# Causal attention with a quantised gate on Trainium2: the gate's closures run at blocks 0, 1, 3, 4 instead of 0, 2, 4, 5

## The chip, the cores and the metric

One Trainium2 chip, 8 cores, one program on all of them. Core 2b and core 2b+1 compute batch element b, each one half of the output features (8 of the 16 heads). The cores share nothing but memory bandwidth. The metric is the device time of the slowest core in microseconds.

## The reference

Shapes: x is 4 x 4096 x 1024 (float32), 16 heads of 64, FFN weight 1024 x 1024 int8.

```python
xn = layernorm(x)                                   # over 1024
qkv = xn @ W                                        # 1024 x 3072
a = softmax(mask(q @ k.T / 8)); s = a @ v           # causal, 16 heads
x_q = clip(round(xn / (amax(|xn|) / 127)))          # per row, int8
g = silu((x_q @ weight_q.T) * x_scale * weight_scale + bias)
out = x + s * g
```

The reference's reshape of k (heads x 64 x sequence read as heads x sequence x 64) is a fixed rearrangement of k, which the kernel makes when it writes `kTa`.

## The kernel before

**Order by hand.** The kernel writes one list of instructions for each engine (`Sched.emit`) with explicit semaphore waits, and replays the lists. So the order of `emit` calls in Python is the order in each engine's queue; nothing is reordered later. An instruction that waits holds up all that its engine has behind it.

**Phases.** First (up to about 590 us) a pass over the 32 row tiles of 128: statistics, normalised tile, transposes, all of k (into `kTa`), and for the first 4 chunks of 512 rows also their quantised tiles. Then attention, chunk by chunk: `emit_attention_chunk(c)` for c = 0 to 7, 512 query rows each. For the chunks from 4 on, tile work is done inside attention: `a_substeps(tc)` gives a list of steps, with `s` (load x and normalise on POOL), `qa`/`qb` (quantise one half tile: four DVE instructions, L428, L430, L433, L436), `p` (transposes on PE, L481 and L486, into the PSUM buffer `pt`, evacuated by DVE at L491), then the row of scales (L512), v (L551), and the FFN (L581, evacuated by DVE L586, then POOL L590, ACT L596, DVE L601). The q projections (L534, evacuated by ACT L540) are a list of their own. The four projections all use the one PSUM buffer `pm`.

**One unit.** Inside a chunk the loop runs over P = 0 to 3 (a pair of heads); this text calls one pass the unit (c,P). A unit has `njb = 4c + 4` blocks `jb` of 128 keys. For each block, in this order in the code: a closure of the previous unit's gate, if this block is in `pops_at`; from block 3 on, the AV pair of the block three before (L788 and L792, into `Oa` and `Ob`, from `eT`); the score pair (L729 and L735; L742 to L767 for the four diagonal blocks) into `sT[par]`, of which there are two; the exp on ACT (L774) from `sT` to one of three `eT`; then `pump()`, which emits usually one step of the tile work, while there is any. The last three AV pairs close the unit. `Oa` and `Ob` are one buffer each, so AV0 of the next unit waits (`O_rd`) until the gate has read them.

**The gate of a unit** is four closures put into `att["pend_gate"]` at the end of the unit and popped in the next one:
- ga1 (`emit_gating_a1`): ACT copies the two rows of softmax sums from `Oa` and `Ob` to `rows` (L821, L824); DVE multiplies `Oa` and `Ob` by the gate `gT` into `wpr` (L827, L831).
- ga2 (`emit_gating_a2`): PE turns the sum rows into columns with fp32 matmuls of one column into `pm` (L842, L846), waiting for the row copies and for `pm`; DVE takes the reciprocal, `linvT` (L852), which frees `pm`.
- gb1 (`emit_gating_b1`): POOL issues the DMA of the residual `xres` (L859).
- gb2 (`emit_gating_b2`): PE transposes `wpr` into `pt` (L870); DVE makes `outs` in eight products (L878, L884), which frees `pt`; POOL issues the output DMA (L891).

`drain_pre` (chunk c, P = 0, block 4c - 1) and `drain_full` (at P = 1) emit whatever of a chunk's own tile work is not out yet. The number of steps that `pump` emits does not depend on the gate. The gate of unit (7,3) is drained after the loop.

Of the kernel before, what the change touches and what calls it, by code (L numbers as in the profile page):

```python
# [67 lines left out]
def build_program(S=4096):  # L68
# [628 lines left out]
    def emit_attention_chunk(c, pump, close_open, drain_pre, drain_full):  # L697
        for P in range(NPAIR):
            if P == 1:
                drain_full()  # L700
            njb = 4 * c + 4
# [5 lines left out]
                if pend_av:  # L707
                    pend_av.pop(0)()

            pops_at = (0, 1, 2, 3) if njb <= 4 else (0, 2, 4, 5)  # L710
            for jb in range(njb):
                if P == 0 and jb == 4 * c - 1:
                    drain_pre()
# [302 lines left out]
    for c in range(NTC):  # L1016
# [37 lines left out]
        def close_open():  # L1054
            drain_open()
        emit_attention_chunk(c, pump, close_open, drain_pre, drain_full)
    while ia["k"] < len(flatA):
        stepA()
# [84 lines left out]
```

How the kernel before makes its waits and increments, by code:

```python
    def replay(self, eng, handle, sems):  # L47
        seen = {}
        own = self.OWN.get(eng)
        prior = 0
        for waits, fn, inc in self.ops[eng]:
            allw = list(waits)
            if own is not None and prior > 0:
                allw.append((own, prior))
            for s, v in allw:
                if seen.get(s, 0) >= v:
                    continue
                handle.wait_ge(sems[s], v)
                seen[s] = v
            ins = fn(handle)
            if inc is not None:
                s, amt = inc
                ins.then_inc(sems[s], amt)
                if s == own:
                    prior += amt
```

## Time and profile before

| | |
|---|---|
| median of 2 runs | 1580.31 us (1579.34 to 1581.28) |
| the profiled execution | 1573.33 us |
| its span, slowest core (core 7) | 1571.8 us |
| spans of the eight cores | 1562.5 to 1571.8 us |
| mean granted TensorE clock, all cores | 0.799 to 0.809 of full speed |
| PE busy | 1112.5 us (71%) |
| ACT busy | 719.3 us (46%) |
| DVE busy | 571.8 us (36%) |
| POOL busy | 299.7 us (19%) |
| DMA | 47.46 MB, mean 30 GB/s |

The rows further down name an engine, a line and an operation with its tiles (out<-in). "[0.45 <-PE sT L735]" at the end of a line of the timeline is the idle time of that engine ahead of the instruction and what ended it. "x2" at the end is the number of instructions merged in one line.
### The profile page before, as it was taken

The numbers are of one execution on the slowest core, as the hardware profiler recorded it, in microseconds if no ns is written. First come the engines' busy times: TensorE is split into PE (matmuls) and PEld (weight loads), VectorE is DVE, ScalarE is ACT, GpSimd is POOL, SyncE is SP. The second block draws the span as 40 slices with busy tenths as digits, with TensorE's granted clock in tenths as the row PEclk, the third lists the DMA queues.
The fourth block names the chain that finished last, engine by engine and source line by source line (L and its number), as shares of the span: only waits on it lengthen the run. The fifth ranks groups of instructions, "written<-read, shape, count | busy, mean of one in ns | idle before, by whom it ended". The sixth has DMA issues, their size and how long they took to land.

```text
span 1571.8 us, 17863 instructions; the slowest of 8 cores (1562.5 to 1571.8 us)
## 1 busy us (share of the span) xinstructions
PE 1112.5 (71%) x5200; PEld 456.6 (29%) x5200; DVE 571.8 (36%) x1086; ACT 719.3 (46%) x905; POOL 299.7 (19%) x412
## 2 busy tenths in 40 slices
PE   0336546445465558996987987888698888888886
PEld 0112212212221214443443433333233333332332
DVE  0484382562735553237237227222721001110000
ACT  0121220211311113553454475467447878888886
POOL 1440430411505451122022022011200000000000
PEclk9956757659586656867988998898798999999998
DMA  7110010000101211021011011001000000000000
GB/s 118 49 33 13 21 34 0 30 24 1 47 7 54 67 47 53 28 67 54 7 48 41 8 48 53 8 21 41 21 8 21 14 14 14 15 22 13 7 14 20
DMA packets 24463, 47.46 MB, mean 30 GB/s; under 512 B 4272, under 2 KB 7472, under 8 KB 24368
## 3 DMA queue, kind: packets, MB, share of 16 engines
q0 software_dynamic: 8816, 20.98, 5.4%
q1 hardware_dynamic: 15552, 25.34, 5.3%
q8 instruction: 44, 0.72, 0.2%
q14 instruction: 51, 0.42, 0.1%
HBM read 40.54 MB, written 8.39 MB: 31 GB/s over the span
## 4 chain that ended last, share of the span: by engine, by line
PE 34%; DVE 26%; ACT 18%; issue 8%; POOL 6%; DMA 6%; DVEq 1%; ACTq 0%; POOLq 0%; SPq 0%
ACT eT L774 16%; PE pm L551 4%; PE Oa L788 4%; PE pm L534 4%; DVE t_r L430 3%; DVE t_b L433 3%; PE Ob L792 3%; DMA xst<-x 3%; PE sT L729 3%; PE pm L581 3%; DVE t_g L428 2%; DMA w8n<-w 2%; PE pm L842 2%; DVE bnst L240 2%; PE pm L846 2%
## 5 line engine op out<-in xcount | busy, mean ns | idle before, releaser
L774 ACT ACTIVATE eT<-sT 128x1024 bf16<-128x1024 f32 (+1 forms) x576 | 548.9, 953 | 271.7 <-PE sT L735 144.8
L788 PE MATMUL Oa<-eT,v_aug 128*65 128x512 bf16 (+1 forms) x576 | 240.1, 417 | 2.9 <-DVE wpr L831 0.2
L792 PE MATMUL Ob<-eT,v_aug 128*65 128x512 bf16 (+1 forms) x576 | 227.8, 400 | 0.0
L729 PE MATMUL sT<-qT,kTa 64*128 64x512 bf16 x448 | 183.4, 418 | 38.7 <-ACT eT L774 37.6
L735 PE MATMUL sT<-qT,kTa 64*128 64x512 bf16 x448 | 186.2, 424 | 0.0
L891 POOL DMA_DIRECT2D out<-outs x32 | 24.2, 756 | 762.2 <-DVE outs L884 705.2
L827 DVE TENSOR_TENSOR wpr<-Oa,gT 64x512 bf16<-64x512 f32 x32 | 21.8, 683 | 363.4 <-PE Ob L792 362.6
L301 PE MATMUL sT<-Wqk,xnK 128*128 128x512 bf16 x256 | 112.0, 616 | 47.3 <-ACT xnK L289 42.8
L729 PEld LDWEIGHTS sT<-qT,kTa 64*128 64x128 bf16 x448 | 40.3, 94 | 225.3 <-issue 222.6
L788 PEld LDWEIGHTS Oa<-eT,v_aug 128*65 128x65 bf16 x576 | 67.7, 118 | 106.8 <-issue 95.5
L551 PE MATMUL pm<-Wv,xnq 128*128 128x512 bf16 x256 | 74.8, 445 | 21.9 <-DVE v_aug L558 17.6
L581 PE MATMUL pm<-xnq,wqT 128*128 128x512 bf16 x256 | 70.2, 424 | 24.6 <-DVE g1s L586 20.5
L281 PE MATMUL pt<-idb_s,xnbf 128*128 128x128 bf16 x128 | 17.3, 283 | 96.4 <-POOL xqbf L269 83.8
L289 ACT ACTIVATE xnK<-pt 128x1024 bf16<-128x1024 bf16 x32 | 32.8, 1024 | 100.0 <-PE pt L281 93.9
L240 DVE BATCH_NORM_STATS2 bnst<-xst 128x6 f32<-128x512 f32 x64 | 44.4, 694 | 90.0 <-DMA xst<-x 84.5
L590 POOL TENSOR_SCALAR t_b<-g1s,wscb,biab 128x512 f32<-128x512 f32 x32 | 24.6, 767 | 271.5 <-DVE g1s L586 271.5
L305 ACT ACTIVATE ktmp<-sT 128x512 bf16<-128x512 f32 x32 | 19.1, 598 | 124.6 <-PE sT L301 124.6
L842 PE MATMUL pm<-idf_s,rows 1*128 1x1 f32 x256 | 50.8, 265 | 34.7 <-DVE wpr L831 22.8
L878 DVE SCALAR_TENSOR_TENSOR outs<-pt,linvT,xres 128x64 f32<-128x64 bf16 x128 | 36.2, 283 | 107.0 <-PE pt L870 93.5
L534 PE MATMUL pm<-xnq,Wqk 128*128 128x512 bf16 x256 | 63.5, 393 | 16.0 <-ACT qT L540 8.7
L792 PEld LDWEIGHTS Ob<-eT,v_aug 128*65 128x65 bf16 x576 | 69.9, 121 | 7.2 <-issue 0.5
L301 PEld LDWEIGHTS sT<-Wqk,xnK 128*128 128x128 bf16 x256 | 32.6, 136 | 106.7 <-issue 106.0
(122 smaller groups left out, 1571.6 us busy)
## 6 DMA issues: line engine op xcount, KB each, us to landing
xst<-x SPq DMA_DIRECT2D x96, 256.0 KB, 2.9
xres<-xr POOLq DMA_DIRECT2D x32, 256.0 KB, 3.6
out<-outs POOLq DMA_DIRECT2D x32, 256.0 KB, 2.8
Wqk<-wq POOLq DMA_DIRECT2D x1, 1024.0 KB, 13.4
Wqk<-wk POOLq DMA_DIRECT2D x1, 1024.0 KB, 24.7
Wv<-wv POOLq DMA_DIRECT2D x1, 1024.0 KB, 29.6
w8n<-w POOLq DMA_DIRECT2D x4, 256.0 KB, 2.6
wscb<-wsc SPq DMA_DIRECT2D x4, 0.5 KB, 6.3
```

The source lines that it names most:

```text
L240: sc.emit("vector", lambda v, buf=buf, h2=h2, bnst=bnst: v.bn_stats(bnst[:, 6 * h2:6 * h2 + 6], xst[:, 512 * buf:512 * buf + 512]), waits= ...
L301: c_mm = sc.emit("tensor", lambda t, kk=kk, xK=xK, slotA=slotA: t.matmul(slotA, xK[:, kk, :], Wqk[:, kk, 512:1024], start=(kk == 0), stop= ...
L430: sc.emit("vector", lambda v, off=off, inv=inv, txn=txn: v.scalar_tensor_tensor(t_r[:], txn[:, off:off + 512], inv, t_g[:], ALU.mult, ALU. ...
L534: c_mm = sc.emit("tensor", lambda t, kk=kk, f=f: t.matmul(pm[:], Wqk[:, kk, 128 * f:128 * f + 128], xnq[:, kk, :], start=(kk == 0), stop=( ...
L551: c_mm = sc.emit("tensor", lambda t, kk=kk, vs=vs: t.matmul(pm[:], xnq[:, kk, 128 * vs:128 * vs + 128], Wv[:, kk, :], start=(kk == 0), sto ...
L581: c_mm = sc.emit("tensor", lambda t, kk=kk, oc=oc: t.matmul(pm[:], wqT[:, kk, 128 * oc:128 * oc + 128], xnq[:, 8 + kk, :], start=(kk == 0) ...
L729: t.matmul(sT[par][:, o:o + w], kTa[0:64, P, 128 * jb:128 * jb + 128], qT[P][0:64, qb + o:qb + o + w], start=True, stop=True), waits=w0)
L735: qb=qb: t.matmul(sT[par][:, 512 + o:512 + o + w], kTa[64:128, P, 128 * jb:128 * jb + 128], qT[P][64:128, qb + o:qb + o + w], start=True, ...
L774: s.activation(eT[pe3][:].rearrange("p (b n) -> p b n", b=2)[:, :, o:o + w], sT[par][:].rearrange("p (b n) -> p b n", b=2)[:, :, o:o + w], ...
L788: sc.emit("tensor", lambda t: t.matmul(Oa[:, o:o + w], v_aug[:, jb, 65 * hA:65 * hA + 65], eT[pe3][:, o:o + w], start=(jb == 0), stop=(jb ...
L792: c_av = sc.emit("tensor", lambda t: t.matmul(Ob[:, o:o + w], v_aug[:, jb, 65 * hB:65 * hB + 65], eT[pe3][:, 512 + o:512 + o + w], start=( ...
L842: c_lt = sc.emit("tensor", lambda t, it=it: t.matmul(pm[0:128, 2 * it:2 * it + 1], rows[64:65, 128 * it:128 * it + 128], idf[64:65, 64:65] ...
```

## The change

The blocks at which the four closures of the previous unit's gate are popped. Units of chunk 0 (4 blocks) keep theirs; the 28 units of chunks 1 to 7 pop ga1, ga2, gb1, gb2 at blocks 0, 1, 3, 4, where it was 0, 2, 4, 5.

```diff
@@ -707,7 +707,7 @@
                 if pend_av:
                     pend_av.pop(0)()
 
-            pops_at = (0, 1, 2, 3) if njb <= 4 else (0, 2, 4, 5)
+            pops_at = (0, 1, 2, 3) if njb <= 4 else (0, 1, 3, 4)
             for jb in range(njb):
                 if P == 0 and jb == 4 * c - 1:
                     drain_pre()
```

So ga2 stands in PE's queue behind the scores of block 0 (and the step pumped there) instead of behind those of block 1; gb1 and gb2 are each one block and one pumped step earlier in the queues of POOL, PE and DVE.

## Rows read from the trace of the kernel before

**Rows 1.** The page's costliest groups: busy, mean ns, idle before and its releaser
```profile
L774 ACT ACTIVATE eT<-sT 128x1024 bf16<-128x1024 f32 (+1 forms) x576 | 548.9, 953 | 271.7 <-PE sT L735 144.8
```

**Rows 2.** Busy us (instructions) by window, then PE clock, DMA share, GB/s
```profile
849.00:988.00 139.00, 114.22 (x605) 51.15 (x603) 59.94 (x108) 74.73 (x85) 21.58 (x28) 0.87 0.10 31
...
1440.00:1572.00 132.00, 107.44 (x506) 39.55 (x504) 15.36 (x44) 99.18 (x104) 5.24 (x7) 0.90 0.05 15
```

**Rows 3.** Timeline of ACT, start of unit (7,1): start, us, engine, line, operation
```profile
1440.12 0.59 ACT L821 ACTIVATE rows<-Oa 1x512 f32<-1x512 f32 x1 [0.57 <-PE Ob L792]
...
1441.48 2.14 ACT L774 ACTIVATE eT<-sT 128x1024 bf16<-128x1024 f32 x2
1444.08 1.02 ACT L774 ACTIVATE eT<-sT 128x1024 bf16<-128x1024 f32 x1 [0.45 <-PE sT L735]
1445.61 1.02 ACT L774 ACTIVATE eT<-sT 128x1024 bf16<-128x1024 f32 x1 [0.51 <-PE sT L735]
1447.14 2.18 ACT L774 ACTIVATE eT<-sT 128x1024 bf16<-128x1024 f32 x2 [0.51 <-PE sT L735]
```

**Rows 4.** Timeline of PE, the same stretch
```profile
1440.13 0.38 PE L729 MATMUL sT<-qT,kTa 64*128 64x512 bf16 x1
...
1441.64 0.35 PE L842 MATMUL pm<-idf_s,rows 1*128 1x1 f32 x2 [1.13 <-DVE wpr L831]
...
1443.20 0.36 PE L846 MATMUL pm<-idf_s,rows 1*128 1x1 f32 x2
1443.49 0.43 PE L729 MATMUL sT<-qT,kTa 64*128 64x512 bf16 x1
...
1444.85 0.60 PE L729 MATMUL sT<-qT,kTa 64*128 64x512 bf16 x1
...
1446.92 0.47 PE L870 MATMUL pt<-idb_s,wpr 128*128 128x128 bf16 x4
```

**Rows 5.** Windows behind the gates run in (7,1) and (7,2)
```profile
1443.56:1447.12 3.56, 3.56 (x13) 0.81 (x14) 0.21 (x1) 2.11 (x3) 0.00 (x0) 0.52 0.00 0
1447.12:1479.00 31.88, 27.86 (x134) 8.92 (x134) 2.26 (x8) 27.39 (x28) 1.49 (x2) 1.00 0.06 17
...
1481.20:1488.10 6.90, 6.90 (x28) 3.76 (x29) 0.21 (x1) 4.02 (x5) 0.00 (x0) 0.51 0.01 2
```

**Rows 6.** Timeline of ACT, start of unit (7,2)
```profile
1484.47 1.02 ACT L774 ACTIVATE eT<-sT 128x1024 bf16<-128x1024 f32 x1 [1.77 <-PE sT L735]
...
1488.97 2.14 ACT L774 ACTIVATE eT<-sT 128x1024 bf16<-128x1024 f32 x2 [0.41 <-PE sT L735]
```

**Rows 7.** The waits: who waited for whom, us in total, times, longest
```profile
PE pt L481 <- DVE outs L884: 30.0, 5, 7.1
...
PE pm L842 <- DVE wpr L831: 22.8, 20, 1.7
```

**Rows 8.** Timeline of DVE and PE, start of unit (4,0)
```profile
947.03 0.48 DVE L428 TENSOR_SCALAR t_g<-t_xn,statq 128x512 int32<-128x512 f32 x1
...
948.80 0.60 PE L729 MATMUL sT<-qT,kTa 64*128 64x512 bf16 x1
...
950.09 0.21 DVE L852 RECIPROCAL linvT<-pm 128x8 f32<-128x8 f32 x1
...
959.67 0.26 PE L481 MATMUL pt<-idb_s,xnK 128*128 128x128 bf16 x1 [6.19 <-DVE outs L884]
...
961.20 0.69 DVE L491 COPY xnq<-pt 128x1024 bf16<-128x1024 bf16 x1 [1.68 <-PE pt L486]
```

**Rows 9.** Timeline of PE, start of unit (3,2)
```profile
893.63 1.89 PE L581 MATMUL pm<-xnq,wqT 128*128 128x512 bf16 x8 [0.69 <-DVE g1s L586]
...
897.07 0.35 PE L842 MATMUL pm<-idf_s,rows 1*128 1x1 f32 x2 [1.56 <-DVE g1s L586]
...
900.69 3.57 PE L581 MATMUL pm<-xnq,wqT 128*128 128x512 bf16 x8
```

**Rows 10.** The page's DMA issues: count, KB each, median us to landing
```profile
xres<-xr POOLq DMA_DIRECT2D x32, 256.0 KB, 3.6
```

## The prediction

> **What bounds the kernel now.** I read the page's groups first, then busy time by stage, then the waits, then the timeline around single gates. "Unit (c,P)" is one pass of the `jb` loop; "the gate" of a unit is its four closures, which run inside the next unit. scN, expN, AVN are the scores, exp and AV pair of jb = N.
>
> The exp (L774) is the costliest group: 548.9 us busy in 576 instructions, 271.7 us idle before them [rows 1]. By stage [rows 2]: in the last 132 us (chunk 7) ACT is busy 99.2 us and PE 107.4, nothing else is near, and DVE has 44 instructions; between 849 and 988 us (chunk 3) the tile work of a later chunk is mixed in, DVE has 108 instructions and 59.9 us. So there are two kinds of stretch: exp-bound units, and units in which PE and DVE hand tiles to each other.
>
> In an exp-bound unit ACT hardly waits away from the two ends: exps follow each other every 1.07 us [rows 3], and in the 31.88 us behind the start of unit (7,1) 28 of them are busy for 27.39 us, PE at full clock [rows 5]. The start of a unit is different. The last AV ends, ACT copies the two sum rows (0.59 us each), then runs exp0 and exp1 from 1.36 us on [rows 3]. PE does sc0 and sc1 at once, then stands until it may run ga2: its 16 fp32 matmuls start 1.52 us after the first row copy and are over at about 3.4 [rows 4]. The wait is 1.13 us here, and of this kind there are 20, together 22.8 us [rows 7]. sc2 comes after ga2, so exp2 waits 0.45 us; then the clock is at its lower level (0.52 of 2.4 GHz, that is 1.2) for some 3.5 us [rows 5], PE needs 1.5 us a block, and exp3 and exp4 wait 0.51 us each [rows 3].
>
> **The change, part by part.** Nothing is added or removed. In the 28 units with c >= 1 three closures come one block earlier; the three gates inside chunk 0 and the drained last gate are as before. ga1 stays.
>
> *ga2 from ahead of sc2 to ahead of sc1, exp-bound unit.* It can't start sooner: the row copies and the two wpr products end at the same moments, and its start follows them, not sc1 [rows 3, 4]. So sc1 (0.22 us at full clock) moves from a hole in PE to behind ga2, and exp1, which ran back to back with exp0, now waits. I walk unit (7,1), zero being 1440.12:
> - before: sc1 0.01, ga2 1.52 to 3.37, sc2 3.37, exp2 3.96, sc3 4.73, exp3 5.49, exp4 7.02, gapless from there [rows 3, 4].
> - after: ga2 1.52 to 3.37, sc1 3.37, exp1 3.96 to 4.98. sc2 follows at 3.7 and exp2 at 5.03 (ACT decides), AV0 takes its 1.0 us (the 1.36 between sc2 and sc3 less the score pair), sc3 stands at 5.2, exp3 at 6.1. The wpr transposes (L870, 0.3 us at full clock, 0.4 at half) now come before AV1 instead of before AV2; AV1 takes 1.0, so sc4 is at about 7.1 and exp4 at 7.65, by then at full clock. exp4 before: 7.02. Loss 0.63 us.
> - unit (7,2) is the other form: the low clock lasts 6.9 us instead of 3.56 [rows 5] and exp2 waits 1.77 [rows 6]. Counted from the start of its old exp2, exp5 starts at 4.50 [rows 6]. The same walk puts exp1 at 0, exp2 at 1.07, sc3 1.3, exp3 2.1, sc4 3.3, exp4 4.0, exp5 5.1: loss 0.6 us.
>
> What is lost in ACT isn't given back, since ACT runs gapless behind it. There are 13 such gates (run in (3,3), (4,2), (4,3), from (5,2) on all): 13 x 0.62 = 8.1 us. Bounds of one: at least 0.22 us (one score pair at full clock, if ACT absorbs all else), at most 1.07 us (a whole exp pitch: exp2's old place taken by exp1, with nothing won back afterwards).
>
> *The same, PE-bound short units.* The gates run in (1,1), (1,2), (1,3) and (2,3) have no tile work either, but PE sets their pace, largely at half clock. The idle stretch of PE grows by sc1, which is then done at either clock: 0.22 to 0.53 us; I take 0.45: 1.8 us.
>
> *Units with tile work in their first blocks* ((2,0), (3,0), (4,0), (5,0) start it, (2,1) and (3,1) end it). Here DVE sets the pace. In (4,0) DVE starts the first quantisation right after wpr, at 947.03, while PE is in ga2; the reciprocal linvT comes after four quantisation instructions, at 950.09 [rows 8]. After the change linvT is queued ahead of them and waits for ga2's end (sc2 starts at 948.80): four instructions start at about 949.1 instead, 2.1 us later, of which 0.3 is linvT itself, no longer in its old slot: DVE loses 1.8. Against this, gb2's eight products (L878, L884) go ahead of the third quantisation (four instructions, 3.1 us, by the distance from the first to linvT) instead of behind it. The tile transposes L481 that wait for them lose less (6.19 us before), and DVE no longer idles 1.68 us before it can evacuate them (L491) [rows 8]. Net 0.1 us lost by these rows, up to 0.5 where that gap is shorter. PE is some 1.3 us earlier at L481, but its next transposes wait for L491, which DVE does no earlier. I take 0.3 for each of the four and 0.3 for the two others together: 1.5 us.
>
> *Units with projections between the first blocks* (five gates: (1,0), (2,2), (3,2), (4,1), (5,1)). ga2 shares pm with them, and each user waits for the evacuation of the one before. In (3,2): L581, sc1, a second L581 at 893.63, 1.56 us of wait, ga2, sc2, the third L581 at 900.69 [rows 9]. After: L581, ga2 at 893.6 in the place of the second L581, sc1, the second L581 at about 896.5 (behind linvT, which stands behind L601 on DVE), sc2, its evacuation, the third L581 at about 899.5: 1.2 us won. I take -1.2 for it and -0.5 for (1,0), which has the same order; (2,2) and (5,1) lose the score pair, 0.25 each; (4,1) is even. Together -1.2 us.
>
> *gb1 and gb2.* The distance from the residual's DMA issue to its user stays one block, in POOL's queue the issue passes at most one step, and without tile work it is issued long before. Cost nothing beyond what is counted; if POOL is behind (it may be with projections) DVE waits for the landing, 3.6 us after the issue [rows 10], as before; both ends of that cost stay under one landing.
>
> **Sum:** 8.1 + 1.8 + 1.5 - 1.2 = 10.2 us. The profiled execution took 1573.3 us (span 1571.8), 7 us under the median of the runs; I add the sum to that median of 1580.3: 1590.5.
>
> **Rivals.**
> - *The stall behind outs is what counts (not slower).* PE waits 30.0 us in five places for L884 to free pt [rows 7]. gb2 one quantisation earlier frees it 3 us sooner, so 15 us could be won: 10.2 - 15 = -5: 1575.5. For it: these are PE's longest waits, and exp waits with them. Against: DVE has hardly a gap behind them, so PE only waits at the next transposes. It turns the sign once more than 2 us of each stays won. Chance 0.16.
> - *The clock stays low longer.* At each gate PE now stands 0.2 us more, with almost no work from the last AV to the end of ga2. Where the low clock lasts 6.9 instead of 3.56 us, exp2 waits 1.3 us more [rows 3, 5, 6]. I take the longer form for about half of the 17 plain gates now, as for one of the two shown; if the others took it too, 8 x 1.3 = 10 us: 1601. Against: work behind ga2 is unbroken in both orders, and the form seems to depend on where ga2 falls. The Trainium skill (TensorE: Matmul & The Clock Gate, Part 1) says that the throttled state is the default and sustained activity releases it; by that rule a longer hole speaks for this rival, and the trace agrees so far that the clock falls at these gates. Chance 0.13.
> - *The whole exp is lost.* 17 x 1.07 + 1.5 - 1.2 = 18.5 us: 1599. It would need PE to win nothing back between sc2 and sc5, though sc2 follows sc1 at once. Chance 0.05.
> - *Forecast*, 1583 to 1598 alone: 0.66.
>
> **How the numbers follow.** Two per cent, about what a measurement of this kernel can tell from no change, is 31.6 us, or 1.13 us for each of 28 gates, above the 1.07 of a whole exp; it needs the second and third rival together. A gain of that size has no source. Faster 0.01, same 0.95, slower 0.04. Lower end: 17 x 0.22 = 3.7, with 1 us won in each of the four tile units and -1.7 for the projections: about -2, 1578. Upper end: the clock rival, with its bound a little over: 1603. Outside stay most of the first rival and the tails of the others, 0.2 in all.
>
> **What would show it.** Each plain unit of the changed kernel has one exp between the row copies and the first wait, exp1 waiting about 1.5 us for L735 and exp2 none; the unit (7,1) is 0.6 us longer. L842 still starts 1.5 us after L821. In (4,0) linvT stands directly behind wpr, with 2 us of DVE idle before it, and L481's wait for L884 falls to about 5 us or less with DVE's end of the tile no earlier. Chunks 6 and 7 grow by 0.6 us a unit; chunks 1 to 4 by little. I am wrong if chunks 6 and 7 don't grow, if the low-clock stretches behind gates grow longer, or if the tile units end earlier than before.

## The result: 1.3% slower

The changed kernel takes 1600.72 us (median of 11 runs) against 1580.08 us (10 runs of the kernel before). The ratio of the runs is 1.0134, 95% interval 1.0111 to 1.0156: 17.5 to 24.6 us more, 21 us in the middle. The direction was the forecast one and the time lies inside the range, but the loss is twice the forecast 10.2 us.

The profiled execution took 1603.33 us, its span is 1601.8. The spans and clocks of the cores (here the shortest, the longest and the medians) show that it isn't one core's trouble:

```profile
core 2: 1585.2 us, clock 0.803
core 3: 1601.8 us, clock 0.795
...
die 0 (median of its cores): 1594.8 us, clock 0.803
die 1 (median of its cores): 1588.8 us, clock 0.798
```

The exp's group on the page, which answers to [rows 1] (busy, mean ns, idle before and its releaser): ACT does the same work and idles 28.3 us more, and the part of it that scores from L735 ended has grown by 28.7.

```profile
L774 ACT ACTIVATE eT<-sT 128x1024 bf16<-128x1024 f32 (+1 forms) x576 | 549.2, 953 | 300.0 <-PE sT L735 173.5
```

The waits, for [rows 7]. ACT's wait for the scores was 144.8 us. ga2 (L842) still waits for wpr in 20 places, 26.8 us for 22.8, so it starts no earlier. PE's wait for outs has indeed fallen, from 30.0 to 19.3 us. And DVE's wait in linvT, which now stands ahead of DVE's other work, is 85.9 us in 29 places, for 72.7 in 27 before:

```profile
ACT eT L774 <- PE sT L735: 173.5, 109, 6.5
...
DVE linvT L852 <- PE pm L846: 85.9, 29, 4.4
...
PE pm L842 <- DVE wpr L831: 26.8, 20, 1.7
...
PE pt L481 <- DVE outs L884: 19.3, 5, 5.3
```

**Where the time went.** In every kernel here the first row copy of each gate (L821) marks the start of a unit. The table takes the lengths of all units so found, as the mean over the eight cores of one profiled execution, and shows the difference to the kernel before, in us, in the kinds of the prediction (e5: cores 0 to 3 alone, against all eight of before, since the other die's clock records stand at 0.81 of full speed for 227 to 332 us of that execution). The last column is another measure: the mean span of the eight cores in all the runs that the ratio is taken from, less the same of the kernel before beside them (for after, less 1572.5 us, that of the 46 runs of the kernel before in the experiments).

| | 13 exp-bound units | 4 short | 6 with tile work | 5 with projections | chunk 0 and the end | sum | mean span, all runs |
|---|---|---|---|---|---|---|---|
| forecast | +8.1 | +1.8 | +1.5 | -1.2 | 0 | +10.2 |  |
| after | +11.0 | +0.5 | +8.9 | +0.2 | +1.3 | +21.9 | +19.4 |
| e1, ga2 only | +9.0 | +0.8 | +9.2 | -1.6 | +1.1 | +18.5 | +14.8 |
| e2, gb1 and gb2 only | +2.7 | -3.6 | +0.4 | -0.5 | +0.8 | -0.2 | -1.7 |
| e3, late linvT | +9.7 | +1.5 | +0.1 | -0.2 | +1.8 | +12.9 | +8.3 |
| e4, after with fillers | -3.1 | +1.1 | +10.1 | +2.1 | +0.7 | +10.9 | +6.7 |
| e5, before with fillers | -17.0 | +1.8 | +1.3 | +0.9 | +1.5 | -11.5 | -18.7 |
| e6, mixed | -18.0 | +2.3 | -0.3 | -0.5 | +1.2 | -15.3 | -18.3 |
| e9, gb2 back in two units | +11.2 | +0.6 | +6.3 | -0.1 | +1.2 | +19.2 | +14.5 |
| e10, both mended | +10.4 | +1.7 | -3.6 | -1.2 | +1.3 | +8.6 | +5.5 |

The exp-bound units and the units with tile work carry the loss. Two things part the sums from the times. The time of a run is that of its slowest core. And the profiled execution of the kernel before, from which every difference is taken, was a short one: its mean span is 1568.9 us, where the 46 other runs have 1568.7 to 1581.5, 1572.5 on average. Against a usual run every sum is thus some 3.6 us too high, and with that taken off, all but e5's agree with the last column within 2.1 us. The short units move by some us from core to core and kernel to kernel and carry no argument.

**Exp-bound units.** ACT at the start of unit (7,1) on the slowest core, for [rows 3]:

```profile
1465.28 0.59 ACT L821 ACTIVATE rows<-Oa 1x512 f32<-1x512 f32 x1 [0.57 <-PE Ob L792]
...
1466.64 1.02 ACT L774 ACTIVATE eT<-sT 128x1024 bf16<-128x1024 f32 x1
1470.77 3.26 ACT L774 ACTIVATE eT<-sT 128x1024 bf16<-128x1024 f32 x3 [3.11 <-PE sT L735]
1474.45 3.26 ACT L774 ACTIVATE eT<-sT 128x1024 bf16<-128x1024 f32 x3 [0.42 <-PE sT L735]
```

There is one exp behind the row copies, and the next one waits 3.11 us; then three run gapless, since their scores are ready. PE, for [rows 4]:

```profile
1465.06 0.39 PE L729 MATMUL sT<-qT,kTa 64*128 64x512 bf16 x1
...
1466.80 0.35 PE L842 MATMUL pm<-idf_s,rows 1*128 1x1 f32 x2 [1.35 <-DVE wpr L831]
...
1469.52 0.56 PE L846 MATMUL pm<-idf_s,rows 1*128 1x1 f32 x2
1470.01 0.60 PE L729 MATMUL sT<-qT,kTa 64*128 64x512 bf16 x1
```

ga2 (eight matmuls, 16 records) starts 1.52 us after the row copy as before. But here the clock fell while it ran: its last pair starts 4.24 us after the row copy, for 3.08 before, and sc1 follows at 4.73 (it stood at 0.01). Whole units (7,1) and (7,2), first of after, then of before (us, then busy time of PE, PEld, DVE, ACT, POOL, and the clock):

```profile
1465.30:1506.50 41.20, 35.65 (x164) 13.27 (x162) 3.85 (x11) 32.68 (x35) 1.49 (x2) 0.92 0.05 13
1506.50:1547.40 40.90, 35.62 (x164) 13.48 (x162) 3.84 (x11) 32.66 (x34) 1.49 (x2) 0.92 0.05 14
```

```profile
1440.10:1479.20 39.10, 33.95 (x164) 11.75 (x162) 3.84 (x11) 32.67 (x34) 1.49 (x2) 0.96 0.05 14
1479.20:1519.60 40.40, 35.52 (x164) 13.05 (x162) 3.84 (x11) 32.68 (x35) 1.49 (x2) 0.92 0.04 14
```

Both units of after have clock 0.92 and take 41.2 and 40.9 us; before, (7,1) has 0.96 and 39.1, (7,2) 0.92 and 40.4. So two things differ: 0.5 us at the same clock, and one more unit with the longer stretch of low clock. Counted over all cores and the 13 units (104 cases), the low clock lasts more than 5 us in 49 cases before (the long form; the others are the short one) and in 74 after. By form, unit (6,2) takes 34.4 (short form) before and 35.0 after, (7,2) 40.4 (long form) before and 40.9 after; over the units that show a form in both kernels it is 0.6 us more on average in the short form (0.5 to 0.8) and 0.4 to 0.5 in the long one (0.1 to 0.7, and 1.2 in (4,2)). That makes some (30 x 0.6 + 74 x 0.4) / 8 = 6 us for the order, and (74 - 49) / 8 = 3.1 more long forms at 1.6 us (36.0 against 34.4 in (6,3) before) = 5 us: together the measured 11.0. The 49 come from that short execution, so the second part is more likely too large than too small.

**Units with tile work.** DVE at the start of (4,0), for [rows 8]:

```profile
960.48 0.68 DVE L831 TENSOR_TENSOR wpr<-Ob,gT 64x512 bf16<-64x512 f32 x1
964.33 0.21 DVE L852 RECIPROCAL linvT<-pm 128x8 f32<-128x8 f32 x1 [3.16 <-PE pm L846]
964.64 0.49 DVE L428 TENSOR_SCALAR t_g<-t_xn,statq 128x512 int32<-128x512 f32 x1
...
970.76 0.28 DVE L878 SCALAR_TENSOR_TENSOR outs<-pt,linvT,xres 128x64 f32<-128x64 bf16 x1
...
973.87 0.49 DVE L428 TENSOR_SCALAR t_g<-t_xnB,statq 128x512 int32<-128x512 f32 x1
974.46 0.75 DVE L430 SCALAR_TENSOR_TENSOR t_r<-t_xnB,statq,t_g 128x512 f32<-128x512 f32 x1
975.33 1.08 DVE L433 SCALAR_TENSOR_TENSOR t_b<-t_r,t_g 128x512 f32<-128x512 f32 x1
976.51 0.90 DVE L436 SCALAR_TENSOR_TENSOR w8n<-t_r,t_b 128x512 bf16<-128x512 f32 x1
977.52 0.69 DVE L491 COPY xnq<-pt 128x1024 bf16<-128x1024 bf16 x1
```

After wpr it idles for 3.16 us in front of linvT (the clock fell under ga2 here too), the first quantisation starts 4.97 us after the row copy (959.67 on this core) instead of 1.60, outs at 11.09 where it was at 11.08. The third quantisation, which now comes last, takes 3.54 us instead of 2.94 (its L433 and L436 1.08 and 0.90 us for 0.69 each), and L491 comes at 17.85 for 15.77: DVE is 2.1 us behind at that point. In two of the eight cores the clock stayed up while ga2 ran in (4,0); there the wait is 2.15 us and L491 comes at 16.8, 1.0 behind. Over the four units that start a tile and all cores, ga2 takes 1.91 us at full clock, and over 2.5 (3.54 at most) in 15 of 32 cases of after and 11 of before; before, DVE had other work meanwhile. DVE of the kernel before, at the third quantisation and at the next one:

```profile
954.91 0.69 DVE L433 SCALAR_TENSOR_TENSOR t_b<-t_r,t_g 128x512 f32<-128x512 f32 x1
955.70 0.69 DVE L436 SCALAR_TENSOR_TENSOR w8n<-t_r,t_b 128x512 bf16<-128x512 f32 x1
...
962.69 1.08 DVE L430 SCALAR_TENSOR_TENSOR t_r<-t_xnB,statq,t_g 128x512 f32<-128x512 f32 x1
963.89 1.06 DVE L433 SCALAR_TENSOR_TENSOR t_b<-t_r,t_g 128x512 f32<-128x512 f32 x1
```

The slow ones stand beside work of POOL in both kernels (L421 and L363 from 961.67 on in before, L421 from 975.98 on in after), the 0.69 ones beside none.

### The profile page after: what moved, and what is told of

Its sections match the earlier page's. It is cut to its first block, busy times and chain, and to the rows that moved or that the text cites. A ratio compares the mean times of both kernels' runs of the same rounds, so it can differ in the third digit from the quotient of the medians.

```text
span 1601.8 us, 17865 instructions; the slowest of 8 cores (1585.2 to 1601.8 us)
## 1 busy us (share of the span) xinstructions
PE 1130.8 (71%) x5200; PEld 467.9 (29%) x5200; DVE 573.0 (36%) x1086; ACT 719.6 (45%) x905; POOL 300.9 (19%) x412
## 4 chain that ended last, share of the span: by engine, by line
PE 35%; DVE 26%; ACT 18%; issue 8%; DMA 5%; POOL 5%; DVEq 1%; ACTq 0%; POOLq 0%; SPq 0%
ACT eT L774 16%; PE pm L551 4%; PE Oa L788 4%; PE pm L534 4%; DVE t_r L430 3%; DVE t_b L433 3%; DMA xst<-x 3%; PE Ob L792 3%; PE sT L729 3%; PE pm L581 3%; PE pm L842 3%; DVE t_g L428 2%; PE pm L846 2%; DMA w8n<-w 2%; DVE bnst L240 2%
## 5 line engine op out<-in xcount | busy, mean ns | idle before, releaser
L729 PE MATMUL sT<-qT,kTa 64*128 64x512 bf16 x448 | 189.0, 432 | 41.3 <-ACT eT L774 39.7
L735 PE MATMUL sT<-qT,kTa 64*128 64x512 bf16 x448 | 191.9, 438 | 0.0
L581 PE MATMUL pm<-xnq,wqT 128*128 128x512 bf16 x256 | 73.8, 440 | 24.1 <-DVE g1s L586 19.9
L842 PE MATMUL pm<-idf_s,rows 1*128 1x1 f32 x256 | 55.5, 284 | 41.7 <-DVE wpr L831 26.8
L842 PEld LDWEIGHTS pm<-idf_s,rows 1*128 1x128 f32 x256 | 49.7, 239 | 51.5 <-issue 51.5
```

The source lines that it names most:

```text
L581: c_mm = sc.emit("tensor", lambda t, kk=kk, oc=oc: t.matmul(pm[:], wqT[:, kk, 128 * oc:128 * oc + 128], xnq[:, 8 + kk, :], start=(kk == 0) ...
L729: t.matmul(sT[par][:, o:o + w], kTa[0:64, P, 128 * jb:128 * jb + 128], qT[P][0:64, qb + o:qb + o + w], start=True, stop=True), waits=w0)
L735: qb=qb: t.matmul(sT[par][:, 512 + o:512 + o + w], kTa[64:128, P, 128 * jb:128 * jb + 128], qT[P][64:128, qb + o:qb + o + w], start=True, ...
L842: c_lt = sc.emit("tensor", lambda t, it=it: t.matmul(pm[0:128, 2 * it:2 * it + 1], rows[64:65, 128 * it:128 * it + 128], idf[64:65, 64:65] ...
```

## The experiments

All ran beside the kernel before, and each ratio is to those runs; after itself was not run again beside them. Differences in unit times are those of the table.

### e1 and e2: ga2 alone, gb1 and gb2 alone

```diff
e1:
-            pops_at = (0, 1, 2, 3) if njb <= 4 else (0, 1, 3, 4)
+            pops_at = (0, 1, 2, 3) if njb <= 4 else (0, 1, 4, 5)
e2:
-            pops_at = (0, 1, 2, 3) if njb <= 4 else (0, 1, 3, 4)
+            pops_at = (0, 1, 2, 3) if njb <= 4 else (0, 2, 3, 4)
```

Expected of e1:

> Only ga2 moved (blocks 0, 1, 4, 5). Theory A (what ga2 holds up: sc1 on PE, and the quantisation on DVE behind linvT): the 13 exp-bound units keep their loss (0.5 us each at the same length of low clock, 0.85 on the mean), the units (2,0), (3,0), (4,0), (5,0) stay 1 to 2 us each over before, while (2,1) and (3,1) lose the part that comes from the eight outs products standing ahead of the copy L518; in all 12 to 16 us over before. Theory B (gb1 and gb2 carry the loss, through pt, xres and DVE's outs): 0 to 6 us over before.

Expected of e2:

> Only gb1 and gb2 moved (blocks 0, 2, 3, 4). Theory A: the exp-bound units are as before within 0.1 us each, (2,1) and (3,1) lose 2 to 3 us each since outs stands ahead of L518, the units that start a tile win up to 1 us each; in all +1 to +6 us. Theory B: 15 us or more over before.

e1: 1.0079 (1.0047 to 1.0111), 12 us over before, as expected. e2: 0.9977 (0.9949 to 1.0005), the same as before or a little under, where 1 to 6 us over it were expected. So the loss comes with ga2, and theory B, that gb1 and gb2 carry it, is out. In the units with tile work the two halves nearly add up (+9.2 and +0.4 for +8.9), in the exp-bound units as well (+9.0 and +2.7 for +11.0). The kinds inside the tile units differ as expected: (2,0), (3,0), (4,0) and (5,0) together are 8.2 us over before in e1 and 4.4 under it in e2. The first miss is (2,1): at 35.4 us in e2 and 33.6 in e1 it seems to lose from gb2, but (2,0) is 25.1 in e2 and 29.2 in e1. DVE works through the boundary, which only moves against it; the pair (2,0)+(2,1) takes 60.6 us before, 62.9 in after, 62.8 in e1, 60.5 in e2. It loses from ga2 alone. The pair (3,0)+(3,1) takes 72.9, 78.1, 75.4 and 75.3: half and half.

PE's wait for outs answers the first rival of the prediction. In e1 and e2 it is:

```profile
PE pt L481 <- DVE outs L884: 34.4, 5, 8.2
```

```profile
PE pt L481 <- DVE outs L884: 9.8, 5, 3.4
```

It falls with gb1 and gb2 from 30.0 us before to 9.8, by 20 us. The four units that start a tile are 4.4 us shorter for it, (2,1) and (3,1) 4.8 us longer, the six together 0.4 us longer. So 20 us in the list of waits were worth 4.4 us where they stood and nothing in the six units together, since DVE set the pace there and L518 came later in (3,1) (e9).

In time the two halves sum to 9 us and after is at 21. With their intervals (about 5 and 4 us either way) and that of after (4 us) the sum may be 3 to 15, so some of after's loss seems to come only with both moves together; the profiled executions show 3.6 us of it (18.5 - 0.2 against 21.9), the mean spans of all runs 6 (14.8 - 1.7 against 19.4). Where it sits isn't settled.

### e3: linvT behind the first quantisation

```diff
             def ga2(c=c, P=P, gst=gst):
+                if P == 3 and 1 <= c <= 4:
+                    c_lt = emit_gating_a2(c, P, gst["lw"][0], True)
+
+                    def rc():
+                        gst["le"] = emit_gating_rc(c_lt)
+                    att["rc"] = rc
+                    return
                 gst["le"] = emit_gating_a2(c, P, gst["lw"][0])
...
                 pump()
+                if att.get("rc"):
...
+                    att["rc"]()
+                    att["rc"] = None
```

The first call emits PE's part of ga2 alone, `emit_gating_rc` the reciprocal.

Expected:

> As after, but in the gates run in (2,0), (3,0), (4,0) and (5,0) the reciprocal linvT is emitted behind the step pumped at block 1 (the first quantisation), not ahead of it; ga2's matmuls stay where after has them. Theory A: DVE starts quantising right after wpr again and these four units shorten by 1.5 us each at least, 5 to 9 us in all with what follows them: 12 to 16 us over before. Rival (the tile units are longer because PE's low clock is longer, not for DVE's order): no more than 2 us faster than after.

1.0036 (1.0004 to 1.0069): 5.7 us over before, 15 less than after by the ratios and 11 less by the mean spans. One DVE instruction of 0.21 us, moved behind four others in four of 32 units, is worth more than half of the loss. The DVE timeline of (4,0), here with linvT at L869, shows the cause gone: quantisation starts 1.58 us after the start of wpr (955.22 on this core), with no idle time, and L491 comes 14.8 us after it instead of 17.8.

```profile
956.01 0.68 DVE L843 TENSOR_TENSOR wpr<-Ob,gT 64x512 bf16<-64x512 f32 x1
956.80 0.48 DVE L428 TENSOR_SCALAR t_g<-t_xn,statq 128x512 int32<-128x512 f32 x1
...
959.86 0.21 DVE L869 RECIPROCAL linvT<-pm 128x8 f32<-128x8 f32 x1
...
970.00 0.69 DVE L491 COPY xnq<-pt 128x1024 bf16<-128x1024 bf16 x1
```

The six units lose 0.1 us instead of 8.9. That is the gain that was expected (5 to 9 us), and so is the sum of 12.9 over before; the time is better than the expected 12 to 16 us over before, in part because the sums are taken against a short execution. The four units also have 6.6 us less low clock than before, where after has 6.4 us more; what share of the gain that is wasn't separated.

### e9 and e10: gb2 back in two units, and both mended

```diff
e9 (e10: with e3's edit as well):
             pops_at = (0, 1, 2, 3) if njb <= 4 else (0, 1, 3, 4)
+            if P == 1 and c in (2, 3):
+                pops_at = (0, 1, 3, 5)
```

In (3,1) of after, outs has slipped ahead of L518, the copy of the scale row, which holds the only buffer (pm) that the q projections wait for. DVE of after, then of before:

```profile
871.68 0.28 DVE L878 SCALAR_TENSOR_TENSOR outs<-pt,linvT,xres 128x64 f32<-128x64 bf16 x1 [0.85 <-PE pt L870]
...
874.40 0.28 DVE L884 SCALAR_TENSOR_TENSOR outs<-pt,linvT,xres 128x64 f32<-128x64 bf16 x1
874.79 0.68 DVE L518 COPY rows<-pm 1x512 f32<-1x512 f32 x1
```

```profile
862.25 0.68 DVE L518 COPY rows<-pm 1x512 f32<-1x512 f32 x1 [1.03 <-PE pm L512]
863.04 0.28 DVE L878 SCALAR_TENSOR_TENSOR outs<-pt,linvT,xres 128x64 f32<-128x64 bf16 x1
```

Expected of e9:

> As after, but in the gates run in (2,1) and (3,1) gb2 is back at block 5 (gb1 stays at 3, ga2 at 1). If the two units are longer because the eight outs products now stand ahead of DVE work that the tile's end needs (the last quantisation in (2,1), the copy L518 in (3,1)), they fall by 3.5 to 5 us together, to about what e1_ga2_only has (33.6 and 42.2), and the whole is 3 to 6 us faster than after, 15 to 18 over before. If they are longer for ga2 or the low clock, they stay at 35 to 36 and 44.

Expected of e10:

> As after, with the late reciprocal of e3_linv_late and gb2 back at block 5 in (2,1) and (3,1). If the losses of DVE's order and of PE's order are separate and add up, only the exp-bound units (+7 to +11), less what the tile units win (-5), and some 1 us at the end stay: 0 to 6 us over before, 4 us or so under e3_linv_late. If mending one only moves the wait to the next, no faster than e3_linv_late.

e9: 1.0112 (1.0070 to 1.0154), 18 us over before, from few runs, which can't be told from after. Its units can: (3,1) falls from 44.2 to 41.6 us as expected; (2,1) stays at 35.4, so there the place of outs is not what counts, as the pair sums of e1 and e2 say. The six units win 2.6 us, not 3.5 to 5. e10: 1.0048 (1.0019 to 1.0077), inside the expected 0 to 6 us over before within its interval, but not under e3; in its profiled execution the six units are 3.6 us under before and 3.7 under e3. The two parts add up in the units. The time does not show the second one; the mean spans do, with 2.8 us (8.3 against 5.5).

### e4 and e5: the hole ahead of ga2 filled

```diff
                     close_open()
+                    if jb == pops_at[1] and ia["k"] >= len(flatA) and ib["k"] >= len(ib["lst"]):
+                        for f in range(5):
+                            sc.emit("tensor", lambda t: t.matmul(
+                                pm[:], idb[:], Wqk[:, 0, 0:512], start=True, stop=True),
+                                waits=(dep["pm_free"],) if f == 0 else ())
                     att["pend_gate"].pop(0)()
```

e4 is after with this edit; e5 is the kernel before with it, for chunks 3 to 7 only (`c >= 3 and`). The fillers' result is never read: ga2 writes over the columns that it uses.

Expected of e4:

> As after, but with five 512-column bf16 matmuls of no use (into pm, 1.1 us at full clock) ahead of ga2 in every unit that has no pumped work left, so that PE isn't idle between sc0 and ga2. Theory C (the longer hole is what makes the low clock last 6.8 instead of 3.4 us more often): the long form falls from about 70% of the exp-bound units to half or less, 4 us or more faster than after. Rival (the form goes by where ga2 itself falls, the hole doesn't matter): share and time as after, within 2 us, or some us slower where the fillers run at the low clock and delay ga2.

Expected of e5:

> The kernel before (gate closures at blocks 0, 2, 4, 5) with the same five fillers ahead of ga2 in the 13 exp-bound units of chunks 3 to 7. If sc1's place behind ga2 has a price of its own that is not the clock's, these 13 units take 0.4 to 0.7 us less each than in e4_fill_hole, where the clock is mostly high as well: 6 to 9 us less together, and the whole is 5 to 10 us faster than before. If the whole loss of the changed kernel in these units was the clock's, e4_fill_hole and this one have the same unit times within 0.2 us.

e4: 1.0023 (0.9994 to 1.0052), 17 us less than after. e5: 0.9890 (0.9860 to 0.9920), 17 us less than before, from three runs; 5 to 10 were expected. Its 13 units are 14 us shorter than e4's, where 6 to 9 were expected; the clock doesn't fall in 40 of the 52 cases of cores 0 to 3, so more than the order differs. In e4 the long form of low clock is left in 7 of 104 cases, and in 47 the clock doesn't fall at all. In these clean units the order of closures has its own price. e4, unit (7,1), PE, ACT and the whole unit (lines are shifted: L718 is the filler, L848 ga2, L780 the exp):

```profile
1453.23 1.25 PE L718 MATMUL pm<-Wqk,idb_s 128*128 128x512 bf16 x5
1454.53 0.35 PE L848 MATMUL pm<-idf_s,rows 1*128 1x1 f32 x2
```

```profile
1454.48 1.02 ACT L780 ACTIVATE eT<-sT 128x1024 bf16<-128x1024 f32 x1
1456.92 6.60 ACT L780 ACTIVATE eT<-sT 128x1024 bf16<-128x1024 f32 x6 [1.42 <-PE sT L741]
```

```profile
1453.10:1492.20 39.10, 33.95 (x169) 12.12 (x167) 3.84 (x11) 32.63 (x34) 1.49 (x2) 1.00 0.05 14
```

With ga2 in its old place (e6, which has e5's fillers; L720, L850, L782), the same unit and the next:

```profile
1433.60 0.38 PE L737 MATMUL sT<-qT,kTa 64*128 64x512 bf16 x1
...
1434.13 1.03 PE L720 MATMUL pm<-Wqk,idb_s 128*128 128x512 bf16 x4 [0.16 <-issue]
1435.09 0.38 PE L850 MATMUL pm<-idf_s,rows 1*128 1x1 f32 x2
...
1436.96 0.39 PE L737 MATMUL sT<-qT,kTa 64*128 64x512 bf16 x1
```

```profile
1434.95 2.14 ACT L782 ACTIVATE eT<-sT 128x1024 bf16<-128x1024 f32 x2
1437.51 7.71 ACT L782 ACTIVATE eT<-sT 128x1024 bf16<-128x1024 f32 x7 [0.42 <-PE sT L743]
```

```profile
1433.50:1471.70 38.20, 33.66 (x168) 12.03 (x167) 3.85 (x11) 32.64 (x34) 1.49 (x2) 1.00 0.05 15
1471.70:1509.60 37.90, 33.64 (x168) 12.02 (x167) 3.85 (x11) 32.63 (x34) 1.49 (x2) 1.00 0.05 14
```

Clock 1.00 throughout in both. With sc1 ahead of ga2 the first wait of ACT is 0.42 us, with sc1 behind it 1.42; the unit takes 38.2 and 39.1 us, and wherever a unit is free of low clock in both kernels the difference is 1.0 us (33.4 and 34.4 in (6,2), 37.9 and 38.9 in (7,2)). At full clock the change costs a whole exp pitch less 0.07. Under the low clock it costs 0.3 to 0.7, for PE's pace of 1.5 us a block then costs ACT time in either order, and one part of the loss hides in the other.

ga2 still takes 1.9 us of one-column matmuls, but behind 1.25 us of 512-column ones the clock stays up in 47 of 104 cases of e4, and in 76 of e6. The Trainium skill (TensorE: Matmul & The Clock Gate, Part 1) has the throttled state as the default, released by sustained activity; after and e4 agree so far, the clock of unit (7,1) going from 0.92 to 1.00 with nothing changed but useless matmuls.

### e7 and e8: the same two kernels, shifted against the clock

```diff
+            if c == 5 and P == 2:
+                for f in range(8):
+                    sc.emit("tensor", lambda t: t.matmul(
+                        pm[:], idb[:], Wqk[:, 0, 0:512], start=True, stop=True),
+                        waits=(dep["pm_free"],) if f == 0 else ())
             for jb in range(njb):
```

Expected of e7 (before):

> The kernel before with eight fillers (1.8 us of PE) once, ahead of unit (5,2), so that the following gates fall elsewhere against the clock's changes. If the share of the long form of low clock is a matter of the place alone, it may be anything from a third to three quarters here; if it hangs on the order of closures, it stays near the half of before (45% to 55%).

Expected of e8 (after):

> The changed kernel with the same eight fillers ahead of unit (5,2). If the longer hole makes the long form more frequent, its share in the units from (5,3) on stays above that of e7_before_shift, at 65% or more; if the place alone decides, the two may come out in either order.

The count runs over the nine units behind the shift, (5,3) to (7,3), on eight cores, 72 cases. Long forms: before 32, e7 49; after 54, e8 46. From the unshifted to the shifted execution the count moves by 17 in one kernel and by 8 the other way in the other, and shifted, the kernel with the old order has the more of them. So these two don't show that the 5 us that after owes to more long forms in its exp-bound units are due to the longer hole. Nor is it known how far the count moves between two executions of one kernel, since none was profiled twice. Taken together the nine profiled executions without fillers at the gates do lean to the order: of 104 cases, ga2 early has 74, 74, 66, 77, 71 and 60 long forms (after, e1, e3, e9, e10, e8), ga2 at its old place 49, 56 and 60 (before, e2, e7). How much of the rise is the order's stays open. What is due to the order without it is nearly the same in both pairs: the 13 units are 6.8 us longer in e8 than in e7 (+9.1 and +2.3 over before), with 60 long forms in each. One run of each is all there is (1583.28 and 1591.17 us).

### e6: a version that beats both

It has e5's fillers, ga2 at block 2 everywhere, and gb1 and gb2 earlier in the four units that start a tile.

```diff
             pops_at = (0, 1, 2, 3) if njb <= 4 else (0, 2, 4, 5)
+            if P == 0 and 2 <= c <= 5:
+                pops_at = (0, 2, 3, 4)
```

Expected:

> As e5_before_fill, and gb1 and gb2 at blocks 3 and 4 in (2,0), (3,0), (4,0), (5,0) only, ga2 at block 2 everywhere. By the sum of parts: fillers -9, and the four units that start a tile -4.4 as in e2_gb_only, while (2,1) and (3,1) stay as before since L518 isn't held up there: 10 to 15 us faster than before. If the gain of the tile units in e2_gb_only was given back in the next units, no more than 10.

0.9893 (0.9873 to 0.9913), 17 us less than before: within the expected 10 to 15 by its interval, but no better than e5 alone. The swap of gb1 and gb2 in the four units, 4.4 us in e2, is worth 1.6 in the units here (-0.3 against +1.3) and nothing that the times can tell: in e6 the clock was low for 19.9 of the 34.0 us of (3,0), for 11.9 before. The fillers are all of the gain that is shown.

## Why the prediction was wrong

- **ga2 can't start sooner, exp1 waits instead of exp2.** Right: L842 at 1.52 us after L821 in both, one exp ahead of the wait. The wait was 3.11 us in (7,1), not about 1.5, as the clock fell under ga2. (What I called 16 matmuls are eight, in 16 records.)
- **0.62 us for each of 13 gates, 8.1 us.** The mechanism was right and the size nearly so: 0.6 us on average in the short form, 0.4 to 0.5 in the long one, some 6 us. Measured were 11.0, the rest being the rise of long forms from 49 to 74 of 104, one of the signs of being wrong that I had named. That is the second rival's mechanism in size (10 us were given for a full change of form). Whether its cause, the longer hole, is the right one stays open: e7 and e8 don't bear it out, the counts of all executions lean to it, and work in the hole takes the long forms away (7 of 104 left in e4, 2 in e6). The bound of 1.07 us, which the third rival takes, is what the order costs at full clock (1.0, e4 against e6). I had priced the walk only at the clock of the trace before.
- **The tile units, 1.5 us.** This is the step that failed: 8.9 us, the largest part of the miss; 3.9 of it in the four units that start a tile (1.2 forecast), 5.0 in (2,1) and (3,1) (0.3 forecast). The prediction saw linvT go ahead of the quantisation and DVE lose 1.8 us. Then it set against this that DVE's gap ahead of L491 would close, leaving 0.1 us, and took 0.3 a unit. The gap did close, but DVE reached L491 of (4,0) 1.0 us late at full clock and 2.1 where the clock fell. Three things were off. ga2 was priced at full clock; where the clock falls under it DVE waits 3.16 us, not 2. The quantisation that takes the gap's place is 0.6 us slower there, beside POOL. And each unit was looked at up to L491 only, as if the rest were as before, while DVE carries its delay over into the next unit. e3 gives the price of that one instruction's place: 8.8 us in the units, 11 in the mean spans, 15 by the ratios.
- **0.3 us for (2,1) and (3,1) together.** Wrong: +2.2 and +2.7. In (2,1) it is ga2's delay of DVE, carried over. In (3,1) half is gb2's: I counted what it passes on DVE in the units that start a tile, but not in the one that ends it, where outs comes ahead of L518. 2.4 us (e2's pair), 2.6 won back in e9.
- **PE's stall behind outs is not the bound (first rival).** Right. The stall fell by 10.7 us in after and 20 in e2, and the six units with tile work together got no shorter.
- **Projections -1.2, short units +1.8.** +0.2 and +0.5. (3,2) won 0.9 us (1.2 forecast) and (1,0) 0.8 (0.5), but (5,1) and (2,2) lost 1.6 and 0.8 where 0.25 each was given; (5,1) had 2.1 us more of low clock.
- **gb1 costs nothing.** No run here speaks against it; it wasn't moved alone.
- **Chunks 6 and 7 grow by 0.6 us a unit.** 0.5 to 1.8 in seven of eight; (6,0) shrank by 0.5, since its long forms went from seven cores to two.

## What to carry to other kernels

An instruction that is moved forward takes its wait with it: ask, for each engine that has a part of the moved step, what now stands behind that wait, and price it by the wait at the lower clock as well. A long wait on an engine that doesn't set the pace can be worth next to nothing when it shrinks; sum the lengths of whole units, and of neighbours together, before a gain is booked. Look whether the profiled execution of the kernel before is a usual one; here it was 3.6 us short, a third of the forecast. Where PE must stand for about a microsecond ahead of one-column matmuls, a few useless dense ones in the hole can keep the clock up; here they won 17 us in either order of the closures.

## What the runs showed of the hardware that was not expected

- The clock fell at all 104 starts of the exp-bound units before, after a hole of 1.13 us and 1.9 us of one-column fp32 matmuls. Five 512-column matmuls in the hole (1.25 us) left it up in 47 of 104 with ga2 early, in 76 with ga2 at its old place, and made the kernel 1.1% faster.
- The eight cores often go the same way in a unit: (6,1) has the short form on all eight before and the long one on all eight in after, and seven or eight agree in 10 of the 13 units before, in 6 of after. So the 104 cases of one profiled execution aren't 104 samples of the clock's place.
- DVE's quantisation step of four instructions took 2.94 us before and 3.54 us in after for the same half tile of (4,0), where POOL's copies (L421) now run beside it. The next step of before, which has POOL beside it too, is as slow (1.08 and 1.06 us for its L430 and L433). That POOL is the cause wasn't tested.
